# A fused four-layer block on one core: the linear-attention head's sums, its gate steps and its output bias change engines, and its slices change places in the queues

## What is computed

```python
q, k = rope(x @ Wq), rope(x @ Wk)
q_phi, k_phi = elu(q) + 1, elu(k) + 1
beta = clip(sigmoid(x @ Wbeta + bbeta), 0.001, 0.999)     # two decays per head and token
# per token, in order:
M = M * b_t + k_t v_t^T ;  Z = Z * b_t + k_t ;  y_t = (q_t M) / (q_t Z + EPS)
out = y @ Wo + bo
h = x + out ;  return ln_gamma * (h - mean(h)) / sqrt(var(h) + LN_EPS) + ln_beta
```

## Time and profile before

| | |
|---|---|
| time, median of 3 runs | 1553.66 us (1552.38 to 1555.31) |
| profiled execution, its own time | 1556.09 us |
| its span, first to last instruction | 1554.8 us |
| busy in the span | PE 1189.6, DVE 1145.6, ACT 734.7, POOL 707.1 us |
| mean granted TensorE clock | 0.875 of 2.4 GHz |

### The profile page before, as it was taken

The page is one execution under the profiler, slowest core; times in us unless marked ns, Lnnn a source line. Parts: engine busy times, 40 slices in busy tenths (PEclk is TensorE's granted clock), DMA queues, the critical chain, the costliest instruction groups (busy, mean ns, idle before and its releaser), DMA issues.

```text
span 1554.8 us, 18685 instructions
## 1 busy us (share of the span) xinstructions
PE 1189.6 (77%) x5568; PEld 543.2 (35%) x5568; DVE 1145.6 (74%) x3003; ACT 734.7 (47%) x1599; POOL 707.1 (45%) x857
## 2 busy tenths in 40 slices
PE   3415987998888886566848677898989898988873
PEld 1112454555444433223312222333333333333222
DVE  5888646757977987869859787787888788877022
ACT  4644783364332354123230266656565656555741
POOL 7334672556775686446660122123413341334244
PEclk9856998999998988776865698999999999989996
DMA  3000104221110100003125101101021202000010
GB/s 106 0 0 1 46 1 127 83 65 55 39 41 30 33 22 0 0 1 66 35 49 82 24 1 26 35 16 36 4 33 16 35 5 32 4 1 3 1 41 14
DMA packets 33666, 47.02 MB, mean 30 GB/s; under 512 B 5007, under 2 KB 18191, under 8 KB 33263
## 3 DMA queue, kind: packets, MB, share of 16 engines
q1 hardware_dynamic: 30974, 43.84, 12.7%
q10 hardware_dynamic: 2592, 2.00, 0.5%
HBM read 39.14 MB, written 6.68 MB: 29 GB/s over the span
## 4 chain that ended last, share of the span: by engine, by line
PE 30%; DVE 21%; ACT 6%; POOL 4%; issue 4%; DMA 0%; ACTq 0%; DVEq 0%; POOLq 0%
PE PS L653 8%; PE PS L611 5%; PE PS L636 5%; DVE PS L1168 4%; DVE SS L1171 3%; PE PS L698 3%; DVE RB L1085 3%; PE PS L310 2%; ACT RB L1574 2%; PE PS L497 2%; DVE st L740 1%; ACT RB L1581 1%; DVE PS L1065 1%; DVE B L1085 1%; PE PS L678 1%
## 5 line engine op out<-in xcount | busy, mean ns | idle before, releaser
L1574 ACT ACTIVATE RB<-PS 128x512 f32<-128x512 f32 (+3 forms) x768 | 328.2, 497 | 268.9 <-PE PS L636 265.1
L611 PE MATMUL PS<-B 96*128 96x512 bf16 (+3 forms) x768 | 259.7, 361 | 54.8 <-DVE B L1214 23.6
L1823 POOL TENSOR_SCALAR_AFFINE_SELECT RB<-RB 128x512 f32<-128x512 f32 x128 | 81.2, 634 | 414.1 <-ACT RB L1574 414.1
L1168 DVE CUSTOM_DVE_ANT_0 PS<-PS,w_msk 128x128 f32<-128x128 f32 (+3 forms) x512 | 244.2, 506 | 29.3 <-PE PS L611 28.8
L636 PE MATMUL PS<-B 96*128 96x512 bf16 (+3 forms) x768 | 242.8, 339 | 18.5 <-ACT RB L1574 16.9
L1171 DVE TENSOR_REDUCE SS<-PS 128x1 f32<-128x512 f32 x256 | 176.0, 687 | 38.5 <-PE PS L611 37.6
L653 PE MATMUL PS<-RB,B 128*32 128x512 f32 (+3 forms) x1536 | 171.9, 520 | 14.4 <-ACT RB L1581 14.4
L611 PEld LDWEIGHTS PS<-B 96*128 96x128 bf16 x768 | 77.2, 102 | 205.1 <-DVE SS L1168 63.2
L1742 POOL TENSOR_TENSOR RB<-RB,B 128x512 f32<-128x512 f32 x64 | 84.8, 1328 | 98.4 <-DVE RB L978 77.2
L636 PEld LDWEIGHTS PS<-B 96*128 96x128 bf16 x768 | 75.6, 100 | 100.1 <-ACT RB L1574 59.3
L497 PE MATMUL PS<-B,WW 128*128 128x512 f32 x128 | 84.9, 800 | 32.8 <-DVE RB L1085 22.7
(11 more groups left out here) (243 smaller groups left out, 2259.0 us busy)
## 6 DMA issues: line engine op xcount, KB each, us to landing
B<-scrW SPq DMA_DIRECT2D x128, 128.0 KB, 3.0
B<-scrQ SPq DMA_DIRECT2D x72, 128.0 KB
scrQ<-B SPq DMA_DIRECT2D x6, 384.0 KB, 6.4
B<-scrK SPq DMA_DIRECT2D x36, 64.0 KB
X<-in_x SPq DMA_DIRECT2D x8, 256.0 KB, 8.6
out_dram<-X SPq DMA_DIRECT2D x8, 256.0 KB, 3.0
B<-in_w SPq DMA_DIRECT2D x3, 576.0 KB, 4.8
B<-in_zeros SPq DMA_DIRECT2D x9, 128.0 KB
```

The lines of the kernel that those rows point to most:

```text
L611: pe.matmul(p[:, 0:w], qs[u % 3][:, h, 128 * i:128 * i + 128], keys_of(u, h)[:, 512 * c:512 * c + w], start=True, stop=True).then_inc(s["m ...
L1168: ins = dve.tensor_tensor_reduce(p, p, msk[:, 512 - w:512], 1.0, LOWEST, ALU.add, ALU.max, MX[:, u % 2, i, h, c:c + 1])
L1574: act.activation(RB[:, 4 * (step % 3) + z, 0:w], bank(bank_of["score", step, z])[:, 0:w], ACT.Exp).then_inc(s["ex2"], 1)
L1823: pool.affine_select(out=pb, in_=pb, compare_op=ALU.is_ge, fill=0.0, base=0, pattern=[[0, 4], [1, 128]], channel_multiplier=-1).then_inc(s ...
```

## The change

- The sine product is made in place in PSUM, and the sum reads that bank and one row; its bank is lent until the sum is done (`rot_d`).
- ACT makes relu(-x), exp of minus that, and relu(x), one slice later than before (k9, k11). POOL adds the two into the features (k10, k12). DVE's L1007 is gone.
- ACT takes tanh in place in PSUM; DVE clips from PSUM to ±0.998 into BETA in the same slice (k11, k12), and the bank is lent until then. ACT makes 0.5 t + 0.5 in a new `gate_d` one slice later (k12, k13).
- ACT normalizes straight into XA (k5). POOL's four sums with the output bias are gone. PE adds the bias ahead of the output products with one product of a row of ones.
- In the joint steps DVE runs the head slices of v0 between its scans and those of v1 behind the second, each ahead of `gated_m`; PE runs a head slice ahead of its unit's products; ACT runs each head slice behind its own Silu.

```diff
@@ PE head_d
+                    w, half = divmod(k - 7, 2)
+                    if half:
+                        banks.lend(i, s["rot_d"], 2 * g + w + 1)
+                    else:
+                        banks.lend(i, s["t_d"], 4 * g + k - 6)
@@ the decays
-                    banks.lend(i, s["beta_d"], 2 * g + k - 10)
+                    banks.lend(i, s["clip_d"], 2 * g + k - 10)
@@ PE pass_f
+                    pe.matmul(p.rearrange("p (i c) -> p i c", c=128), ones[:, :],
+                              rows[0:1, 0, :].unsqueeze(1).to_broadcast([1, 4, 128]),
+                              start=True, stop=False, skip_group_check=True)
@@ PE joint steps
                 for v in beside(step):
+                    between_m(v)
                     experts(v)
@@ DVE head_d
-                    dve.tensor_tensor(row(q + half), bank(bank_of["pj_d", g, k - 7]),
-                                      cs[:, half, 512 * h:512 * h + 512], ALU.mult).then_inc(s["t_d"], 1)
+                    dve.tensor_tensor(p if half else row(q), p, cs[:, half, 512 * h:512 * h + 512],
+                                      ALU.mult).then_inc(s["t_d"], 1)
...
-                        dve.tensor_tensor(row(q), row(q), row(q + 1), ALU.add).then_inc(s["rot_d"], 1)
+                        dve.tensor_tensor(row(q), p, row(q), ALU.add).then_inc(s["rot_d"], 1)
...
+                    dve.tensor_scalar(BETA[k - 11][:, 512 * g:512 * g + 512], bank(bank_of["pj_d", g, k - 7]),
+                                      -0.998, 0.998, ALU.max, ALU.min).then_inc(s["clip_d"], 1)
@@ DVE joint steps
+                for v in beside(step)[0:1]:
+                    between_m(v)
                 for v in units[0:1]:
                     gated_m(v)
                 if step < 36:
                     memory_c(step, 1)
+                for v in beside(step)[1:2]:
+                    between_m(v)
                 for v in units[1:2]:
                     gated_m(v)
-                for v in beside(step):
-                    between_m(v)
@@ ACT head_d
+                    own.done(act.activation(e, x, ACT.Relu, scale=-1.0))
                     own.wait()
-                    act.activation(row(10 + 2 * w), row(10 + 2 * w), ACT.Relu).then_inc(s["er_d"], 1)
+                    own.done(act.activation(e, e, ACT.Exp, scale=-1.0))
+                    act.activation(x, x, ACT.Relu).then_inc(s["er_d"], 1)
...
+                    act.activation(p, p, ACT.Tanh, scale=0.5, bias=HBB[k - 11]).then_inc(s["beta_d"], 1)
...
+            def gate_d(g, k):
+                if k in (12, 13):
+                    d = BETA[k - 12][:, 512 * g:512 * g + 512]
+                    act.wait_ge(s["clip_d"], 2 * g + k - 11)
+                    act.activation(d, d, ACT.Copy, bias=0.5, scale=0.5).then_inc(s["gate_d"], 1)
@@ POOL head_d
-                if k == 5:
-                    pool.wait_ge(s["hn0"], 16 + g + 1)
-                    for j in range(4):
-                        ins = pool.tensor_tensor(XA[:, 4 * g + j, :], quarter(row(8 + g % 2), j), rows[:, 0, :], ALU.add)
-                    ins.then_inc(s["xb_d"], 1)
+                if k in (10, 12):
...
+                    pool.wait_ge(s["er_d"], 2 * g + w + 1)
+                    pool.tensor_tensor(cf((QD, KD)[w], g), row(11 + 2 * w), row(10 + 2 * w), ALU.add).then_inc(s["ft_d"], 1)
```

More of the change, by code:

```diff
@@ L443, in head_d @@
                     i = next_d(v)
-                    turned(room(i), lambda j: quarter(row(8 + g % 2), j), s["tp0"])
+                    turned(room(i), lambda j: XA[:, 4 * g + j, :], s["tp0"])
                     banks.lend(i, s["xf_d"], g + 1)
@@ L483, in tensor_program @@
                     experts(step - FIRST_UNIT)
+                    between_m(step - FIRST_UNIT)
             for v in range(NG + 15 - FIRST_UNIT, ALONE):
                 experts(v)
+                between_m(v)
             def value_c(n):
@@ L994, in head_d @@
                         dve.wait_ge(s["w_cs"], 16)
-                    dve.tensor_tensor(row(q + half), bank(bank_of["pj_d", g, k - 7]),
-                                      cs[:, half, 512 * h:512 * h + 512], ALU.mult).then_inc(s["t_d"], 1)
+                    p = bank(bank_of["pj_d", g, k - 7])
+                    if half == 0 and g:
+                        dve.wait_ge(s["ft_d"], 2 * g + w - 1)
+                    dve.tensor_tensor(p if half else row(q), p, cs[:, half, 512 * h:512 * h + 512],
+                                      ALU.mult).then_inc(s["t_d"], 1)
                     if half:
                         dve.wait_ge(s["t_d"], 4 * g + k - 6)
-                        dve.tensor_tensor(row(q), row(q), row(q + 1), ALU.add).then_inc(s["rot_d"], 1)
-                if k in (9, 11):
-                    w = (k - 9) // 2
+                        dve.tensor_tensor(row(q), p, row(q), ALU.add).then_inc(s["rot_d"], 1)
+                if k in (11, 12):
                     if g >= 6:
[L1003 to L1014, removed]
+                        dve.wait_ge(s["nm_c"], ROWS_FROM)
+                    dve.wait_ge(s["cf_n"], 8)
+                    dve.wait_ge(s["beta_d"], 2 * g + k - 10)
+                    dve.tensor_scalar(BETA[k - 11][:, 512 * g:512 * g + 512], bank(bank_of["pj_d", g, k - 7]),
+                                      -0.998, 0.998, ALU.max, ALU.min).then_inc(s["clip_d"], 1)
             routes = [route(r) for r in range(3)]
@@ L1431, in head_d @@
                 if k == 5:
-                    if g >= 2:
-                        act.wait_ge(s["tp0"], 16 + g - 1)
-                        act.wait_ge(s["xb_d"], g - 1)
-                    normed(g, "d", x_tile, row(8 + g % 2), s["hn0"])
+                    normed(g, "d", x_tile, tokens(XA, g), s["hn0"])
                 if k == 6:
@@ L1462, in between_m @@
                 for g, k in head_slices(v):
+                    gate_d(g, k)
                     head_d(g, k)
@@ L1674, in gpsimd_program @@
             own.done(pool.memset(mhalf[:, :], -0.5))
+            own.done(pool.memset(ones[:, :], 1.0))
             for b in range(NB):
```

32 lines of the change are left out of this document (18 added, 14 removed).

## The result

The changed kernel takes 1578.12 us (median of 4 runs, 1571.68 to 1582.2) against 1554.1 in the same comparison: ratio 1.0135, interval 1.0105 to 1.0166. By the ratio it is slower by some 21 us (the medians differ by 24.0), and far outside the range. Its profiled execution took 1571.68 us, the shortest of the four (span 1570.2, mean granted clock 0.870), so the two traces can show 15 of the 21 us; the runs of the changed kernel also lie wider apart than those of before.

The account below looks back on a forecast made before the run. PE was taken to bound the units alone, PE and DVE waiting for each other in joint steps 0 to 17. The items, -14.7 + 1.6 + 1.6 - 4.6 + 2.4 + 0.5 = -13.2 us, gave 1541 us; range 1520 to 1557.

Parts of the forecast that it names:

- item 2: Joint steps 3 and 12: DVE idles 3.8 us as the clip waits for tanh; net +0.6 and +1.0, together +1.6 us.
- item 6: Units alone: PE is full, DVE's saving is worth 0, a clip waiting for tanh costs a little: +0.5 us.
- rival C: Joint steps' six groups: clip waits the full 3.8 us and PE loses it too; +8, 1562 us; chance 0.17 with D.
- Rival D: ACT's table loads on the new path: another 1.4 us lost at each, adding 6 to 8 us, 1548; chance within C's 0.17.
- Item 5: Bias products on PE outside batch 1: 0.5 to 1.0 us each, +2.4 us; removing POOL's additions is worth nothing.
- item 4: Joint steps 19 to 25: step 24 -3.7, steps 19, 20, 25 -1.8, -1.1, -0.8, step 21 +2.8; sum -4.6 us.
- Item 1: Nine ordinary joint steps: PE's projection finds its bank free and `value_c` starts as the second scan ends; -14.7 us.
- Item 3: Batch boundaries, steps 8, 17, 26: next scan waits for POOL's feature sum and ACT's copy; +2.1, -0.8, +0.3, sum +1.6 us.
- Rival A: DVE's saving comes through: 52% of 58 us appears, in all -26 us, 1528; chance 0.25.
- Rival B: PE-bound steps: ordinary steps give only what the other parts cost, some 9 us, so the time stays; chance 0.10.

Follow-up runs that it names:

- e3: The changed kernel with all operations as changed, but the joint steps' order of before on DVE, PE and ACT: 1577.04 us, ratio 1.0135.
- e1: The changed kernel with ACT's tanh in slice k11 moved ahead of the feature steps of that slice, nothing else: 1565.67 us, ratio 1.0061.
- e8: The changed kernel with ACT's tanh ahead of its slice's feature steps and POOL's feature sum of v0 ahead of the recurrence's sum and product: 1557.68 us, ratio 0.9991.
- e12: The changed kernel with the same operations, but ACT's three feature steps and POOL's feature sum each one slice earlier: 1549.56 us, ratio 0.9953.
- e2: The changed kernel with the decays' path as before (tanh into SBUF, two gate steps on DVE, bank lent until the tanh): 1563.52 us, ratio 1.0042.
- e7: The changed kernel without the eight bias products, so the output lacks the bias: 1565.05 us, ratio 1.0048.
- e9: The kernel before with the new order, the sine product and sum in PSUM and the new decays' path; features and bias as before: 1526.09 us, ratio 0.9822.
- e11: The changed kernel without the two bias products of the last batch alone: 1574.41 us, ratio 1.0126.
- e4: The kernel before with the new order of the joint steps alone, all operations as before: 1531.77 us, ratio 0.9837.
- e5: The changed kernel with the features made as before (Exp and Relu on ACT, one DVE step, no POOL sum): 1543.51 us, ratio 0.9913.

## Why the prediction was wrong

**The step that failed first is item 2, with item 6 as the same mistake**: the wait of the clip for the tanh. Its length was right (3.8 forecast, 4.50 and 3.94 for DVE in steps 3 and 12). Its price was not: +1.6 forecast, +9.2 measured for the two steps (step 12 also holds a bias pair, 1.1 us). "PE, busy 13.1 of 13.5, lets it get no shorter" took PE as working on under DVE's wait. But PE's next projection needs bank 7, which is held until the tanh and the clip are done, so PE waited 4.15 us too, and behind the gap it ran at half the clock. e3 shows that this does not hang on the projection's new place ahead of the unit's products. In the units alone "PE is full, +0.5" was the same mistake: the clip held bank 7 for the turn and the next projection, and from unit 20 on the stretch grew by 10.4 us, 6.1 of it more idle time of PE and 4.3 longer work. There the place inside the slice is not the cure: e1, e8 and e12 take 64.5, 65.9 and 62.9 us. Only the old features (56.2) or the old decays' path (58.3 in e2) bring most of it back. Step 16, which was not on the list, grew by 3.2.

This is rival C's mechanism, at fewer places: steps 3 and 12 grew by 3.7 and 5.5 us net, and C's six times 3.8 had nothing for the stretch ahead of the first scan, or for the clock. I gave it 0.17 together with D because PE's place in front of the bank was argued group by group from the list of slices, instead of being followed through bank 7: every projection, and the turn, needs it.

**Item 5 (with the 1.1 us in item 4) is the second step that failed**: 3.5 us forecast, 14 measured, twice (e7 and e9). The products themselves were sized at less than half. All of them in the changed kernel:

```profile
L551 PE MATMUL PS<-w_rows,ones x16: 587/677/1218, 514.6 to 896.5; 1*128 1x512 f32 x16
```

They stand as 16 rows, two for each of the eight products. I had taken a product as one row, 0.5 to 1.0 us, when the earlier trace rows shows the two value products as four. A pair takes 1.1 to 1.5 us up to batch 2 and 2.07 in the last batch; the eight add up to 11.3 us, where item 5 and step 21 had 3.5. By the traces of e7 and the changed kernel the price is not where those of batch 0 stand: joint steps 0 to 17 take 239.9 and 240.1 us. Steps 18 to 26 take 3.8 us less without the bias, steps 27 to 34 2.5 and the rest 4.5. The clock's late return in the last batch is a likely part of the last figure, but e11, which should have shown it, did not show it as time.

**Item 1 was right in size, and mostly for the stated reason.** The nine ordinary steps gave 18.6 us where 14.7 was forecast, and 4.9 us came back in steps 5 and 14. The order alone gives 16.8 of it (e4), and with the changed operations still 9.7 (e3 against the changed kernel). What I missed is that over the whole kernel the order needs the old operations: with the changed ones it gives nothing (e3 equals the changed kernel).

**Item 3 was right**: +2.3, +0.1 and +0.1 in steps 8, 17 and 26, where +2.1, -0.8 and +0.3 stood. But these are sums of a gain and a loss: from e5 to the changed kernel they grow by 13.9. A forecast of the whole step hid that POOL's place behind the recurrence was worth repairing.

**Item 4 failed in step 24** (-3.7 forecast, 0.0 measured); steps 19, 20, 21 and 25 came to -1.4, -0.7, +3.6 and -0.8 for -1.8, -1.1, +2.8 and -0.8, and step 22 grew by 0.9. The sum is +1.6 for -4.6. The steps freed from DVE in step 24 let two later ones start beside POOL. DVE and POOL in the changed kernel:

```profile
701.29 2.92 DVE L895 TENSOR_TENSOR B<-B,w_rows 128x1024 f32<-128x1024 f32 x1
704.24 3.25 DVE L1127 TENSOR_TENSOR XA<-B,w_rows 128x1024 f32<-128x1024 f32 x1
```

```profile
700.79 2.34 POOL L1785 TENSOR_TENSOR RB<-RB 128x1024 f32<-128x1024 f32 x1 [10.95 <-DVE RB L1092]
703.21 3.21 POOL L1787 TENSOR_TENSOR RB<-RB,B 128x1024 f32<-128x1024 f32 x1
```

Before, the same two took 1.21 and 1.22 us, with POOL idle, and it was L999 that took 2.35 beside POOL's recurrence. All four instances of the second, before and after:

```profile
L1120 DVE TENSOR_TENSOR XA<-B,w_rows x4: 1224/1224/3248, 564.9 to 907.7; 128x1024 f32<-128x1024 f32 x4
```

```profile
L1127 DVE TENSOR_TENSOR XA<-B,w_rows x4: 1224/3250/3257, 571.1 to 927.4; 128x1024 f32<-128x1024 f32 x4
```

In the changed kernel the three long ones lie beside POOL's work, and the one of 1.22 does not. So it seems that part of the 86.4 us of the earlier trace rows was contention, not work, and that it moved to what came next: these two lines (up to 830 us) grew by 5.9 us, most of what DVE's busy time fell short of the forecast. The Trainium skill ("SBUF — State Buffer", SBUF: two separate sides) says that a VectorE step with two SBUF inputs and a GpSimd step that reads SBUF need one shared pair of ports, and that whichever starts second waits for the first. The rows agree with it; I had not weighed it. No run here takes POOL's work away from beside these two, so the cause is argued from the traces alone.

**Rival A** (DVE's saving comes through) is refuted as a rule: e9 against e4 takes 27.8 us of DVE work off (1129.7 to 1101.9 busy) for 2 us of time. **Rival D** is not needed: in step 3 the tanh's chain has no gap behind its table load. The rule on PSUM operands held: the clips took 0.66 to 0.69 us. Rival B's sum leaves out the 7.4 us that item 4 takes off outside step 21: by the prediction's own terms the time stays when the ordinary steps give 1.5 us, not 9.

**Still open:** why the order gives nothing together with the changed operations. In e3 the nine ordinary steps are 9.7 us longer than in the changed kernel, and steps 16, 17 and 21 are 6.9 shorter; I have the lengths, not the cause. Open too is why the features one slice earlier bring so little back ahead of the first scan. The start varies from run to run: in e7 and e11, the same program up to there, the first scan came at 375.4 and 374.2. Of that, 7.6 and 6.3 us had already been lost at the Silu of unit 20 (311.6 and 310.3), and from there it took 63.8 and 64.0 us as in the changed kernel's 64.5. So the spread arises ahead of the stretch that the change touches most; its cause isn't known.

## What to carry to other kernels

When a step moves to an idle engine, its price is what it stands behind and what stands behind it there, not its length: here some 28 of 34 us came back by moving three ACT steps and a POOL sum one slice earlier. Follow a shared PSUM bank through every engine's queue before calling a wait covered. Price the order and the operations apart, since their gains need not add: the fastest version measured (e9) keeps the order and leaves features and bias where they were; e4, the order alone, is not told apart from it.

## What the runs showed of the hardware that I had not expected

- A gap of PE of 3.5 to 4.2 us (336.18, 410.09) is followed by about 4 us at a granted clock of 0.50; a gap of 1.2 us at the same place (e12) is not. The products behind the gap then take up to twice as long. A single long gap isn't needed: in e12 gaps of 1.79 and 2.06 us with one projection between them (337.12, 340.31) were followed by 3 us at 0.58.
- At the low clock 8 us of output and bias products, where 2.2 us of output products had stood, go with a clock that is still at 0.50 at 905 us. Why that work doesn't bring the clock back, though PE is busy for 15.2 of the 16 us, isn't shown.
- DVE steps with both inputs in SBUF took 2.4 and 2.7 times as long beside POOL's (1.21 and 1.22 against 2.92 and 3.25); sums with one input in PSUM took 691 to 693 ns in all 16 places.
